# Keys by tokens: one block transposition on VectorE and a trip through DRAM in place of TensorE transposes and PSUM copies

## The reference, cut to what matters

```python
mixed = silu(causal_conv(x_norm @ w_qkv, conv_w))     # 4 taps along the tokens
q, k, v = split(mixed)                                # 16 key heads, 32 value heads, 128 wide
state = state * exp(g_t)
kv    = einsum('bhk,bhkv->bhv', k_t, state)
state = state + einsum('bhk,bhv->bhkv', k_t, (v_t - kv) * b_t)
out   = einsum('bhk,bhkv->bhv', q_t, state)
```

## Time and profile before

| what | value |
|---|---|
| median of 3 runs | 1587.05 us (1585.59 to 1589.31) |
| the profiled execution's own time | 1595.38 us |
| its span | 1593.5 us |
| PE busy, weight loads busy | 1413.3 us (89%), 1003.7 us (63%) |
| DVE busy | 1012.1 us (64%) |
| ACT, POOL busy | 768.7 us (48%), 701.0 us (44%) |
| mean granted PE clock | 0.946 |
| DMA queue of SP | 120880 packets, 17.8% of the 16 DMA engines |

### The profile page before, as it was taken

How to read it: one execution, slowest core, us unless ns; L and a number is a source line. 1 busy time by engine, 2 the same in 40 slices (tenths; PEclk the granted TensorE clock), 3 DMA queues, 4 the chain that set the end, 5 groups by cost and what they waited for, 6 DMA issues and landing times. The chain is left out here.

```text
span 1593.5 us, 26389 instructions
## 1 busy us (share of the span) xinstructions
PE 1413.3 (89%) x9528; PEld 1003.7 (63%) x9528; DVE 1012.1 (64%) x2099; ACT 768.7 (48%) x1800; POOL 701.0 (44%) x1215
## 2 busy tenths in 40 slices
PE   6768899999999999999999999988769789789993
PEld 3456676767767667676677776776535446555672
DVE  5856777777777877778777777775330366461353
ACT  3445556565655656556556575664311155311120
POOL 1673663836638356474654746551100000007254
PEclk9879999999999999999999999999879899979997
DMA  2201111111111111111111111110062170023486
GB/s 77 67 18 38 28 38 37 37 29 34 38 37 35 31 34 38 27 39 38 34 38 24 41 37 35 24 21 14 7 246 101 33 179 1 9 77 106 100 176 152
DMA packets 127154, 86.72 MB, mean 54 GB/s; under 512 B 92403, under 2 KB 113095, under 8 KB 126257
## 3 DMA queue, kind: packets, MB, share of 16 engines
q1 hardware_dynamic: 120880, 76.50, 17.8%
q0 software_dynamic: 6144, 8.53, 2.9%
HBM read 61.65 MB, written 23.76 MB: 54 GB/s over the span
## 5 line engine op out<-in xcount | busy, mean ns | idle before, releaser
L562 PE MATMUL psum_banks<-main_hT,gdn_w_in 128*128 128x512 f32 x512 | 262.2, 640 | 9.5 <-DVE heads_y L941 3.9
L941 DVE SCALAR_TENSOR_TENSOR heads_y<-psum_banks,gdn_conv_w,heads_y 128x1021 f32<-128x1021 f32 (+2 forms) x192 | 245.2, 1278 | 28.1 <-ACT heads_y L791 26.0
L1163 POOL TENSOR_TENSOR heads_XT<-heads_XT,heads_tmp 128x126 f32<-128x126 f32 (+22 forms) x496 | 209.2, 422 | 38.9
L1160 POOL TENSOR_TENSOR heads_tmp<-heads_XT,heads_A 128x126 f32<-128x126 f32 (+22 forms) x496 | 186.3, 376 | 43.5 <-PE psum_banks L726 4.0
L562 PEld LDWEIGHTS psum_banks<-main_hT,gdn_w_in 128*128 128x128 f32 x512 | 95.5, 199 | 97.2 <-issue 79.0
L1141 POOL TENSOR_TENSOR heads_og<-heads_og,heads_fac 128x512 f32<-128x512 f32 x64 | 64.5, 1040 | 178.5 <-DVE heads_fac L1012 178.5
L703 PE MATMUL psum_banks<-heads_w_o,heads_ogT 128*128 128x256 f32 x512 | 120.7, 385 | 3.6 <-ACT heads_ogT L857 3.6
L672 PE MATMUL psum_banks<-heads_w_z,main_hT 128*128 128x256 f32 x512 | 123.6, 385 | 0.3 <-DVE heads_v_s L1031 0.3
L791 ACT ACTIVATE heads_y<-psum_banks,gdn_conv_w 128x1024 f32<-128x1024 f32 x64 | 71.2, 1113 | 100.4 <-PE psum_banks L562 100.0
L1775 POOL DMA_INDIRECT expert_rows<-moe_rows,route_dest x32 | 31.4, 981 | 188.9 <-DVE route_dest L1754 179.5
L809 ACT ACTIVATE heads_O<-psum_banks,heads_coef 128x128 f32<-128x128 f32 x224 | 69.5, 362 | 91.8 <-PE psum_banks L593 90.5
(11 more groups left out here) (256 smaller groups left out, 3070.3 us busy)
## 6 DMA issues: line engine op xcount, KB each, us to landing
main_w_gu<-in_w_gu SPq DMA_DIRECT2D x4, 2816.0 KB, 24.2
gdn_w_in<-in_w_in SPq DMA_DIRECT2D x16, 512.0 KB, 3.5
heads_A<-kk_blocks SPq DMA_DIRECT2D x64, 128.0 KB, 2.7
moe_wd<-in_w_down SPq DMA_DIRECT2D x32, 176.0 KB
expert_rows<-attn_zeros SPq DMA_DIRECT2D x1, 4624.0 KB, 25.4
moe_be<-expert_rows SPq DMA_DIRECT2D x32, 144.5 KB, 3.2
heads_w_z<-in_w_z SPq DMA_DIRECT2D x16, 256.0 KB, 2.7
heads_w_o<-in_w_o SPq DMA_DIRECT2D x16, 256.0 KB, 2.7
```

What stands on the lines that cost most here:

```text
L562: ins = pe.matmul(out[:, half * 512:(half + 1) * 512], w_in[:, kd_, j * P:(j + 1) * P], hT[:, kd_, half * 512:(half + 1) * 512], start=kd_ ...
L941: dve.scalar_tensor_tensor(y[j][:, shift:T], src[:, 0:T - shift], conv_w[:, head, j, t:t + 1], y[j][:, shift:T], ALU.mult, ALU.add).then_i ...
L1160: pool.tensor_tensor(tmp[:, 0:n, 0:m], bc_last(XT[:, 0:n, j], m), bc_mid(A0[:, j, j + 1:BLK], n), ALU.mult).then_inc(solve_step.sem, 1)
L1163: pool.tensor_tensor(XT[:, 0:n, j + 1:BLK], XT[:, 0:n, j + 1:BLK], tmp[:, 0:n, 0:m], ALU.add).then_inc(solve_step.sem, 1)
```

## The change

The products "k0" and "k1" and their copies go. After the silu of head h+1, DVE transposes all of `kT` in one instruction into `y[0]` (`turn_keys`, quantum 7 of step h; head 0's in the preparation, head 1's in quantum 6 of step 0). It transposes inside each 32x32 block only. SP stores `y[0]` to DRAM (512 KB, rows of 4 KB) behind the loads of `A0`, and loads it back at the start of the next step in four DMAs of 128 KB, whose runs of 32 values (128 B) put the blocks in their places; that is 4 x 1024 runs. PE waits for the loads before the first state update that uses them, a step later; ACT waits for the store before it writes `y[0]` again.

```diff
-    [("k0", 1), ("k1", 2)],
+    [],
...
-    "k0", "p0 p1", "norm_q k1", "v0 v1", ...
+    "", "p0 p1", "norm_q", "v0 v1", ...
...
-AT = {"variance": 0, "factors": 7, "turn": 9, "scales": 12, "keys": 3, "norms": 12}
+AT = {"turn_keys": 7, "variance": 0, "factors": 7, "turn": 9, "scales": 12, "keys": 3, "norms": 12}
...
-FIRST_AT = {"turn": 12, "scales": 11, "keys": 3, "norms": 11}
+FIRST_AT = {"turn_keys": 6, "turn": 12, "scales": 11, "keys": 3, "norms": 11}
...
+    kt = nc.dram_tensor("turned_keys", (P, T), F32, kind="Internal").ap()
...
+            def store_turned_keys(h):
+                sp.wait_ge(k_turned.sem, h + 1)
+                if h:
+                    sp.wait_ge(k_tok_loaded.sem, k_tok_loaded.end(h - 1) * 16)
+                sp.dma_start(kt, y[0][:]).then_inc(kt_stored.sem, 16)
+
+            def load_key_rows(h):
+                sp.wait_ge(kt_stored.sem, (h + 1) * 16)
+                src = kt.rearrange("(a i) (c r j) -> r i c a j", i=BLK, r=NB, j=BLK)
+                for r in range(NB):
+                    dst = k_tok[h % 2][BLK * r:BLK * (r + 1)].rearrange("i c (a j) -> i c a j", j=BLK)
+                    sp.dma_start(dst, src[r]).then_inc(k_tok_loaded.sem, 16)
...
             gate_rows(0)
             gate_rows(1)
+            store_turned_keys(0)
+            load_key_rows(0)
...
                 if h in INVERT:
                     wait(sp, a_full, a_full.base(h))
+                    if h:
+                        load_key_rows(h)
                     sp.wait_ge(solve_step.sem, solve_step.end(h))
...
                     key_block_stores(h)
                     load_key_blocks(h + 1)
+                if h in AHEAD:
+                    store_turned_keys(h + 1)
...
                         pe.wait_ge(dt_ready.sem, dt_ready.done(h, f"dt{c}"))
+                        if c == 0:
+                            pe.wait_ge(k_tok_loaded.sem, k_tok_loaded.end(h - 1) * 16)
...
-                elif name.startswith("k"):
-                    for j in range(4):
-                        ins = pe.transpose(bank[b][:, j], kT[h % 3][:, (4 * u + j) * P:(4 * u + j + 1) * P], ident[:])
-                    ins.then_inc(full[b].sem, 1)
...
-                        if j == 1:
+                        if j == 0:
+                            act.wait_ge(kt_stored.sem, kt_stored.base(h) * 16)
+                        elif j == 1:
...
+            def turn_keys(h):
+                dve.wait_ge(k_ready.sem, h + 1)
+                dve.transpose(y[0][:], kT[h % 3][:]).then_inc(k_turned.sem, 1)
...
-                if name in ("k0", "k1"):
-                    dve.wait_ge(full[b].sem, full[b].done(h, name))
-                    dve.tensor_copy(flat(k_tok[par][:, 4 * u:4 * u + 4]), flat(bank[b][:])).then_inc(free[b].sem, 1)
-                elif name == "norm_q":
+                if name == "norm_q":
...
             dve.tensor_copy(q4(G_), by_head(g_c)).then_inc(s_v, 1)
+            turn_keys(0)
...
+                    if h in AHEAD and k == at(h, "turn_keys"):
+                        turn_keys(h + 1)
```

More of the change, by code:

```diff
@@ L239 @@
 FIRST = [[(name, BANK[name]) for name in row.split()] for row in (
-    "k0", "p0 p1", "norm_q k1", "v0 v1", "p2 p3 v2", "v3 kk0 p4 p5", "kk1", "decay0 decay1 decay2 decay3 p6 p7", "attn0",
+    "", "p0 p1", "norm_q", "v0 v1", "p2 p3 v2", "v3 kk0 p4 p5", "kk1", "decay0 decay1 decay2 decay3 p6 p7", "attn0",
     "attn1", "", "", "", "y6a y6b", "u6a u6b", "y7_0", "y7_1 u7_0", "u7_1", "", "", "", "", "")]
@@ L442, in heads @@
     w_o_ready = per_head("w_o_loaded", "w", steps=FINISH)
+    k_turned = per_head("keys_turned", "it", before=1, steps=AHEAD)
+    kt_stored = per_head("turned_keys_stored", "it", before=1, steps=AHEAD)
+    k_tok_loaded = per_head("key_rows_loaded", "0", "1", "2", "3")
     k_ready = per_head("keys_ready", "k", before=1, steps=AHEAD)
@@ L626, in product @@
                 b = BANK[name]
-                if h == 0 and name == "k0":
-                    pe.wait_ge(conv_done.sem, 6)
-                elif h == 0 and name in ("norm_q", "k1"):
+                if h == 0 and name == "norm_q":
                     pe.wait_ge(conv_done.sem, 9)
@@ L632, in product @@
                     pe.wait_ge(w_z_ready.sem, w_z_ready.done(h, "w") * 16)
-                elif name == "k0":
-                    pe.wait_ge(k_ready.sem, k_ready.base(h) - 1)
                 elif name == "kk0":
```

## The result

The changed kernel takes 1580.13 us (median of 20 runs, 1574.73 to 1586.28); the kernel before, beside it on the same chip, 1589.38 (20 runs, 1585.18 to 1595.07). The ratio is 0.9944, with a 95% interval of 0.9930 to 0.9958: 9.3 us faster, where 20.7 were forecast. Three later comparisons gave 0.9914, 0.9926 and 0.9935. So the sign was right, the size was not, and 1580.13 lies 1.1 us above the range.

A forecast was written before the change was run, and what follows sets the result against it. PE's list was nearly full, but DVE set the pace in quanta 4 to 6. Instructions 10.6 plus lower clock 10.1 gave 20.7 us: 1595.38 to 1574.7, less 8.3 for the median, 1566.4 us; range 1558 to 1579.

The forecast's parts named there:

- Transposes out: PE, quanta 4 to 6: removing 8 key transposes a step (1.04 us) gains nothing, since L591 still waits for `S`.
- Copies out: DVE, steps 1 to 15: without the key copies, all behind them comes 1.20 us earlier a step.
- Transposition: DVE, quantum 7, steps 1 to 14: takes 1.23 us, delays `X` by 0.84 and later work by about 0.60 us.
- C: Transposition costs its upper bound, 1.80 us; net 0.03 us a step, 1584.4 us, no change; chance 0.06.
- D: Transposition in quantum 7 waits for POOL's normalisation (1.04 us); a step nets -0.44 us, 1596.6 us, slower; chance 0.05.
- F: Transposition pays its start for every 128 columns, 2.42 us; net -0.59 us a step, 1601.0 us, slower; chance 0.03.
- DMA: Key loads (3.5 us) hidden in SP's wait for POOL, key store behind the `A0` loads: zero cost, upper end 3.5 us.
- Rival E: Key store delays `A0` at L986 by 3.5 us, less 0.48 us slack; 1618 us, slower; chance 0.03.
- The beat of the lower clock: Steps 1 to 15: shorter steps cut stretches at 1.2 GHz from ten to four, 1.69 us each, gaining 10.1 us.
- A: The beat of the lower clock does not carry over, ten stretches stay; only 10.6 us gained, 1576.5 us; chance 0.18.
- B: All ten stretches of lower clock go, PE's transposes being what starves the clock; 27.5 us gained, 1559.6 us; chance 0.08.
- Step 0: PE's path in step 0: removing the second set of key transposes gains about 1.0 us; the first set, zero.

The follow-up runs named there:

- DMA alone: Changed kernel with the block transposition left out of every step, key store and loads kept (keys wrong): ratio 0.9866 to the kernel before.
- filled pair: Kernel before and changed kernel, each with twelve extra 512-column matmuls, results unused, in PE's waits of step 0: 1593.31 and 1574.09 us.

## Why the prediction was wrong

*Transposes out: right.* PE's new wait of 0.92 us for `S` shows that they filled a wait.
*Copies out: right, slightly over.* 1.13 us a step where 1.20 was forecast. In step 15, without transposition, the interval went from 54.53 to 53.97 us: 0.6 instead of 1.20.
*Transposition: right.* It was 1.235 to 1.240 us in all 16 steps (1.23 forecast); PE's wait for `X` 0.64 us (0.8); net 0.53 (0.60). The net gain of a spared step is 0.59, forecast 0.60. Rivals C, D and F fall with the duration, which is the same beside POOL's work (the transposition starts at 591.32 us, POOL's normalisation at 591.48).
*DMA: right.* With and without transfers a step has 64.81 us. The loads are issued from 569.46 and SP's next issue is at 576.65. Rival E falls: in 16 steps DVE waits 4.3 us in all for `A0`, and it waited 3.1 before.

```profile
L1004 DVE STREAM_TRANSPOSE heads_y<-heads_kT x16: 1235/1237/1240, 33.0 to 986.7; 128x1024 f32<-128x1024 f32 x16
```
```profile
569.46 3.05 SPq L510 DMA_DIRECT2D heads_k_tok<-turned_keys  x4
576.65 1.27 SPq L557 DMA_DIRECT2D inverse_blocks<-heads_XT  x2
```
```profile
L1010 DVE TENSOR_SCALAR heads_nd<-heads_A x16: 177/188/192, 42.0 to 1001.4; 128x32 f32<-128x32 f32 x16
...
  DMA heads_A<-kk_blocks: 4.3, 9
```

*The beat of the lower clock: nearly right.* In the changed kernel 4 or 5 of 14 intervals were hit in four profiles (4 of 15 steps forecast), in the kernel before 10, 10 and 8; six fewer were forecast, some five found. Over the fifteen steps between first and last copy of `S` the kernel before took 994.2, 997.0 and 991.2 us, the changed one 978.5, 976.9, 975.5 and 975.5: means 994.1 and 976.6, a gain of 17.5 us. The terms for this stretch were 8.4 + 1.2 + 10.1 = 19.7. Rivals A and B fall. The share goes with the length of the step in the run with two transpositions (65.35 us, six hits) against one in quantum 10 (64.81, one), though there the length is not told from what quantum 7 delays; the run with DMA alone (64.81, four) shows that it is not the length alone.

*Step 0: this step failed.* The prediction put "about 1.0 us" gained there: it priced PE's transposes as instructions on the path and did not ask what their absence does to the clock. In the profiles nothing is gained even in the short course (64.7 us without them, 64.4 with), and the first copy of `S` comes at 107.2 us in the mean of the changed kernel's profiles, at 104.2 before: 2.9 us lost. The changed kernel mostly takes the long course, 2.2 to 2.5 us longer than the middle course and 6 us longer than the short one.

*The step from the profile to the median failed with it.* The 8.3 us by which the profiled execution of the kernel before lay above its median were carried over whole to the changed kernel. They came from what varies in one program. Against the third profiled execution of the same kernel, 13.4 us shorter, the first one has the middle course in place of the short one (3.5 us), a later start of step 0 (2.2), longer steps (3.0) and a longer part behind the last copy of `S` (4.7). The changed kernel's own profiled execution, at 1577.07, has no such excess: it lies 3.1 us below its median, though it took the long course, as three of its four profiles did. In the mean of its four profiles the changed kernel is 14.3 us shorter than the kernel before in the mean of three: 17.5 in the fifteen steps, less 2.9 up to the first copy and 0.4 behind the last. The medians show less. If the kernel before usually takes the short course and the changed one the long, the 17.5 us gained in the steps less 70.3 - 64.4 = 5.9 lost in step 0 leave 11.6; four comparisons gave 9.3 to 11.5 by medians. The up to 2 us between stay open.

How far is this shown? The gain of the steps is read from seven profiles. That step 0's clock eats the other part is supported by the filled pair: with 27.3 us at 1.2 GHz up to the first copy in both, the whole gain appears (19.2 us); one profile of each shows this, and the kernel with quantum 10 did not answer to filling. That the kernel before usually takes the short course is inferred: if both kernels took the same course, the changed one, with some 16 us fewer at 1.2 GHz in its steps (23.9 against 39.8 in the mean of the profiles), would have a median as much lower. On the three chips where both ran it has 154.8 us (22 runs) against 158.8 (81 runs), 4 lower. (In the first comparison its 20 runs have 165.7, and there is no such figure for the kernel before.) So some 12 us at 1.2 GHz came back; the long course has 17.1 more than the short one, the middle one 10.2 more, and the changed kernel seems to take both. In profiles the kernel before took the short course only once in three.

Why the changed kernel takes the longer ones stays open. The missing transposes may take part in it: with them kept, both profiles show the short course, and 3 of 8 runs had 145 us or less at 1.2 GHz, which none of 42 runs of the changed kernel had. But the median did not move (0.9925 against 0.9926). The Trainium skill (TensorE: Matmul & The Clock Gate, Part 4) says that transposes do not count as busy for the clock as matmuls do; two profiles with the transposes and ten without speak against it in this step, but do not settle it.

**The better version.** Transposition in quantum 10 and step 0's transposes kept: 1560.62 us, by the ratio 1.9% under the kernel before (1.7% by the medians, with 1587.33 beside it); the quantum alone gives 1.7% (1.4% by the medians). The difference between the two lies within the intervals, so what the transposes add is not shown.

## What to carry to other kernels

Place an operation that is moved to another engine where that engine idles: the same 1.24 us cost 0.53 in one quantum and nothing three quanta on. Before a term rests on the clock, take two or three profiled executions and cut them at marks that both kernels have; a profile that is slower than every timed run is a warning that one of its stages took an unusual course. And when work is removed from TensorE, look at the granted clock where it stood: a term read from the timeline as a gain of 1.0 us came out as a later start of what follows.

## Not expected of the hardware

The pattern of steps with a stretch at 1.2 GHz is so sensitive that moving the transposition, which shortened a step by 0.54 us (65.35 to 64.81), took most of the remaining hits away, four or five down to one: 14 x 0.54 = 7.6 us were expected of moving the transposition, and the steps between the copies of `S` gave 976.6 - 963.5 = 13.1 us. And one program, the kernel before, took step 0 in 64.4 or in 68.0 us, with 27.3 or 37.5 us at 1.2 GHz up to its end.
